# Mixture-of-experts stage: two experts' first products together, then two experts' second products; eight buffers weighted in place; sums in two banks

## The reference

```python
combine = (one_hot(topk_idx, 8) * softmax(topk_vals)[..., None]).sum(axis=1)   # 2 of 8 experts
h = relu(einsum('td,edh->teh', x_flat, W1) + b1)      # first product, hidden width 128
y = einsum('teh,ehd->ted', h, W2) + b2                # second product
out = einsum('ted,te->td', y, combine)             # weighted sum over the experts
```

## Time and profile before

| | us |
|---|---|
| median of 3 runs | 1169.35 (1168.31 to 1169.48) |
| the profiled execution's own time | 1169.17 |
| its span, first to last instruction | 1167.4 |
| PE busy over the span | 1102.7 (94%) |
| ACT busy | 794.0 (68%) |
| DVE busy | 694.9 (60%) |
| POOL busy | 142.1 (12%) |
| DVE line 2071 (`mult`), 64 | 78.2, mean 1.221 |
| ACT line 1269 (`relu`), 64 | 71.2, mean 1.113 |
| PE line 1679 (`second`), 256 instructions | 68.9 |
| a weight row from issue to landing, median of 64 | 7.8 |

### The profile page before, as it was taken

One profiled execution on the slowest core, in us unless ns is written; L12 is line 12 of the kernel. 1 busy time (PEld: TensorE's weight loads), 2 busy tenths in 40 slices (PEclk: granted clock), 3 DMA queues, 4 the chain that ended last, 5 costly groups with the idle time before them and its releaser, 6 DMA issues.

```text
span 1167.4 us, 62466 instructions
## 1 busy us (share of the span) xinstructions
PE 1102.7 (94%) x26872; PEld 930.9 (80%) x26872; DVE 694.9 (60%) x3130; ACT 794.0 (68%) x4592; POOL 142.1 (12%) x220
## 2 busy tenths in 40 slices
PE   3799999999999999999999999999798699889998
PEld 2699999999999999999999999999544388623332
DVE  7565455555555555555555554444456669899985
ACT  1466677777777777777777777666569888556654
POOL 4200000000000000000000000000104212412110
PEclk9555555555555555555555555555699989999999
DMA  5000000000000000000000000000000000448675
GB/s 141 8 9 9 9 12 11 10 9 9 9 14 10 9 9 9 14 10 9 9 5 4 5 4 4 4 4 5 2 1 1 1 1 1 147 160 287 216 261 173
DMA packets 30545, 47.20 MB, mean 40 GB/s; under 512 B 12274, under 2 KB 21563, under 8 KB 30268
## 3 DMA queue, kind: packets, MB, share of 16 engines
q1 hardware_dynamic: 30268, 43.21, 11.1%
HBM read 40.84 MB, written 2.36 MB: 37 GB/s over the span
## 4 chain that ended last, share of the span: by engine, by line
PE 83%; DVE 8%; ACT 4%; issue 2%; POOL 2%; DMA 1%; SPq 0%; DVEq 0%; ACTq 0%
PE bank L659 44%; PE bank L756 7%; PE bank L1386 5%; PE bank L739 5%; PE bank L1679 4%; PE bank L427 4%; PE bank L528 3%; PE bank L734 2%; PE bank L751 1%; DVE gp L2071 1%; POOL stat L1027 1%; PE bank L1584 1%; PE bank L412 1%; PE bank L1419 1%; PE bank L447 1%
## 5 line engine op out<-in xcount | busy, mean ns | idle before, releaser
L659 PE MATMUL bank<-space,whh_hi 128*128 128x8 f16 x16384 | 612.4, 170 | 7.2 <-DVE space L787 4.6
L659 PEld LDWEIGHTS bank<-space,whh_hi 128*128 128x128 f16 x16384 | 530.6, 105 | 28.0 <-DVE space L787 8.2
L787 DVE TENSOR_TENSOR space<-h_f,space 128x16 f16<-128x16 f32 x2048 | 290.6, 176 | 384.3 <-ACT h_f L768 383.0
L768 ACT ACTIVATE h_f<-bank 128x16 f32<-128x16 f32 x2048 | 298.5, 183 | 234.5 <-PE bank L659 228.4
L774 ACT ACTIVATE space<-bank 128x16 f16<-128x16 f32 x2048 | 298.0, 183 | 1.1 <-PE bank L659 1.1
L756 PE MATMUL bank<-space,wih_hi 128*128 128x32 f16 x2048 | 178.2, 188 | 0.0
L659 PE MATMUL bank<-space,whh_lo 128*128 128x32 f16 (+1 forms) x2096 | 145.2, 191 | 0.0
L739 PE MATMUL bank<-xr,wih_lo 128*128 128x32 f16 x512 | 123.6, 241 | 0.0
L427 PE MATMUL bank<-onehot,tab 128*128 128x128 f16 x448 | 116.7, 266 | 0.4 <-DVE prepare_cur L477 0.4
L756 PEld LDWEIGHTS bank<-space,wih_hi 128*128 128x128 f16 x2048 | 114.2, 104 | 0.0
L739 PE MATMUL bank<-xr,wih_hi 128*128 128x32 f16 x512 | 109.8, 215 | 0.0
(11 more groups left out here) (288 smaller groups left out, 1560.8 us busy)
## 6 DMA issues: line engine op xcount, KB each, us to landing
space<-weights_kept SPq DMA_DIRECT2D x64, 512.0 KB, 7.8
space<-in_x SPq DMA_DIRECT2D x28, 129.0 KB, 3.1
out<-res SPq DMA_DIRECT2D x8, 256.0 KB, 9.6
space<-in_wrec SPq DMA_DIRECT2D x1, 768.0 KB, 4.2
space<-in_wx SPq DMA_DIRECT2D x1, 740.5 KB, 9.4
brec<-in_brec SPq DMA_DIRECT2D x1, 260.0 KB
ew<-in_ew SPq DMA_DIRECT2D x1, 256.0 KB, 4.1
weights_kept<-wturned SPq DMA_DIRECT2D x8, 32.0 KB, 1.8
```

What stands on the lines that cost most here:

```text
L659: mm = pe.matmul(own[:, m, :], w[:, k, m * P:(m + 1) * P], steps(h, k), start=False, stop=False, skip_group_check=True)
L768: act.activation(h_f[layer][:, s % 2, :, :], own, ACT.Tanh, scale=scale[layer]).then_inc(s_h[layer], 1)
L787: dve.tensor_tensor(h[layer][:, :, s % RINGS[layer], 1, :], h_f[layer][:, s % 2, :, :], h[layer][:, :, s % RINGS[layer], 0, :], ALU.subtra ...
```

## The change

Six edits, all in the last stage:

1. PE takes slots in pairs (2k, 2k + 1): `hidden(2k + 2)`, `hidden(2k + 3)`, then `weights_turned` if due, `second(2k - 1)`, `second(2k)`, then the norm, gates or `sum_turned` of either slot.
2. `relu` and `mult` share eight buffers (`gel`, `gp`, and two old attention tiles, two slots each). `mult` writes over what it reads. `relu(n)` waits for `second(n - 8)` and no longer for a `mult`; `mult(n)` no longer waits for a `second`.
3. The expert sums of even sequences go to bank 2, of odd ones to bank 7; `second` waits for the copy of two sequences ago.
4. `sum_turned` writes to bank 3, which the norm also uses; the norm waits for `add_experts` of the sequence before, `sum_turned` for the norm's copy.
5. SP issues weight row e only when row e - 3 of the same sequence has landed.
6. The queues of ACT and DVE keep their order.

```diff
--- before.py
+++ after.py
@@ -902,7 +902,9 @@
         grank, gsel, gc = (tmp(n, [P, TT, NE]) for n in ("grank", "gsel", "gc"))
         gleft, wturned = tmp("gleft", [P, NE, TT]), tmp("wturned", [NE * TT, P])
         gr = gel[:, :, :, :].rearrange("p e h t -> p e (h t)")
-        weighted = gp[:, :, :, :].rearrange("p e h t -> p e (h t)")
+        gr_more = gp[:, :, :, :].rearrange("p e h t -> p e (h t)")
+        expert_at = lambda n: (gr, gr_more, rabs, phk)[n % 8 // 2][:, n % 2, :]
+        sum_bank = lambda b: bank[2 + b % 2 * 5]
         gst = tmp("gst", [P, 3, TT])
         wide = rph.rearrange("p (e t) -> p e t", e=NE)
         weight_rows = whole[0:NE, :]
@@ -947,6 +949,8 @@
                 if x == 0:
                     sp.wait_ge(s_phi, B)
                 for e in range(NE):
+                    if e >= 3:
+                        sp.wait_ge(s_wide_row[e - 3], 16 * (x + 1))
                     if x:
                         sp.wait_ge(s_gp, NE * (x - 1) + e + 1)
                     sp.dma_start(wide[:, e, :], kept[x, e].partition_broadcast(P)).then_inc(s_wide_row[e], 16)
@@ -1264,16 +1268,16 @@
 
             def relu(n):
                 act.wait_ge(s_hid, n + 1)
-                if n >= 2:
-                    act.wait_ge(s_gp, n - 1)
-                act.activation(gr[:, n % 2, :], banks[n % 2 * 2][:, :], ACT.Relu, bias=ebias[:, n % NE:n % NE + 1],
+                if n >= 8:
+                    act.wait_ge(s_sec, n - 7)
+                act.activation(expert_at(n), banks[n % 2 * 2][:, :], ACT.Relu, bias=ebias[:, n % NE:n % NE + 1],
                                scale=unscale[S_E1]).then_inc(s_r, 1)
 
             def sum_copy(b):
                 act.wait_ge(s_sec, NE * (b + 1))
                 if b:
                     act.wait_ge(s_moet, b)
-                act.activation(yt[:, :], bank[2], ACT.Copy).then_inc(s_moec, 1)
+                act.activation(yt[:, :], sum_bank(b), ACT.Copy).then_inc(s_moec, 1)
 
             for b in range(B):
                 if b == 6:
@@ -1664,30 +1668,30 @@
             def second(n):
                 b, e = divmod(n, NE)
                 if e == 0:
-                    if b:
-                        pe.wait_ge(s_moec, b)
+                    if b == 0:
+                        pe.wait_ge(s_lg, 2)
+                    elif b == 1:
+                        pe.wait_ge(s_wor, B)
                     else:
-                        pe.wait_ge(s_lg, 2)
+                        pe.wait_ge(s_moec, b - 1)
                     pe.wait_ge(s_wgt_rows, 16 * (b + 1))
                     for half in range(2):
-                        mm = pe.matmul(bank[2][half * D:(half + 1) * D, :], eb2[0:NE, :],
+                        mm = pe.matmul(sum_bank(b)[half * D:(half + 1) * D, :], eb2[0:NE, :],
                                        weight_rows[:, half * 512:(half + 1) * 512], start=True, stop=False,
                                        skip_group_check=True)
                     mm.then_inc(s_b2, 1)
                 pe.wait_ge(s_gp, n + 1)
                 for half in range(2):
-                    mm = pe.matmul(bank[2][half * D:(half + 1) * D, :], ew2[:, e, :], gp[:, n % 2, half, :],
-                                   start=False, stop=(e == NE - 1), skip_group_check=True)
+                    mm = pe.matmul(sum_bank(b)[half * D:(half + 1) * D, :], ew2[:, e, :],
+                                   expert_at(n)[:, half * 512:(half + 1) * 512], start=False, stop=(e == NE - 1),
+                                   skip_group_check=True)
                 mm.then_inc(s_sec, 1)
 
             def sum_turned(b):
                 pe.wait_ge(s_moec, b + 1)
-                if b:
-                    pe.wait_ge(s_fin, b)
-                else:
-                    pe.wait_ge(s_wor, B)
+                pe.wait_ge(s_xt, OPEN + B + min(b + 3, B))
                 for i in range(4):
-                    mm = pe.transpose(bank[7][:, i * P:(i + 1) * P], yt[:, i * P:(i + 1) * P], eye[:, :])
+                    mm = pe.transpose(bank[3][:, i * P:(i + 1) * P], yt[:, i * P:(i + 1) * P], eye[:, :])
                 mm.then_inc(s_moet, 1)
 
             for b in range(B):
@@ -1718,22 +1722,32 @@
                 project_out(b)
             gates(1, bank[2][:, 0:TT * NE])
 
-            for n in range(slots):
-                b, e = divmod(n, NE)
-                y, step = divmod(n + 3, NE)
-                if n + 1 < slots:
-                    hidden(n + 1)
-                if step == 7 and y + 1 < B:
-                    weights_turned(y + 1, bank[6][0:NE * TT, P:2 * P])
-                if n:
-                    second(n - 1)
-                if step == 0 and y + 1 < B:
-                    norm_turn(pe, bank[3], B + y + 1)
-                elif step == 1 and y + 1 < B:
-                    gates(y + 1, bank[6][:, 0:TT * NE])
-                if e == 3 and b:
-                    sum_turned(b - 1)
+            hidden(1)
+            for k in range(slots // 2):
+                pair = (2 * k, 2 * k + 1)
+                for n in pair:
+                    if n + 2 < slots:
+                        hidden(n + 2)
+                for n in pair:
+                    y, step = divmod(n + 3, NE)
+                    if step == 7 and y + 1 < B:
+                        weights_turned(y + 1, bank[6][0:NE * TT, P:2 * P])
+                for n in pair:
+                    if n:
+                        second(n - 1)
+                for n in pair:
+                    b, e = divmod(n, NE)
+                    y, step = divmod(n + 3, NE)
+                    if step == 0 and y + 1 < B:
+                        if b:
+                            pe.wait_ge(s_fin, b)
+                        norm_turn(pe, bank[3], B + y + 1)
+                    elif step == 1 and y + 1 < B:
+                        gates(y + 1, bank[6][:, 0:TT * NE])
+                    if e == 3 and b:
+                        sum_turned(b - 1)
             second(slots - 1)
+            pe.wait_ge(s_fin, B - 1)
             sum_turned(B - 1)
 
 
@@ -2062,18 +2076,15 @@
 
             def mult(n):
                 b, e = divmod(n, NE)
-                if n == 1:
-                    dve.wait_ge(s_att, B)
-                elif n >= 2:
-                    dve.wait_ge(s_sec, n - 1)
+                own = expert_at(n)
                 dve.wait_ge(s_r, n + 1)
                 dve.wait_ge(s_wide_row[e], 16 * (b + 1))
-                dve.tensor_tensor(weighted[:, n % 2, :], gr[:, n % 2, :], wide[:, e, :], ALU.mult).then_inc(s_gp, 1)
+                dve.tensor_tensor(own, own, wide[:, e, :], ALU.mult).then_inc(s_gp, 1)
 
             def add_experts(b):
                 dve.wait_ge(s_moet, b + 1)
                 own = res[:, span(b), 0:D].rearrange("p (h i) d -> p h i d", h=2)
-                dve.tensor_tensor(own, halves(bank[7]), own, ALU.add).then_inc(s_fin, 1)
+                dve.tensor_tensor(own, halves(bank[3]), own, ALU.add).then_inc(s_fin, 1)
 
             for n in range(slots):
                 b, e = divmod(n, NE)
```

## The result

| | before | changed |
|---|---|---|
| median of 13 runs each | 1169.82 (1168.31 to 1171.38) | 1171.95 (1170.72 to 1173.71) |
| ratio to before, 95% interval | | 1.0019 (1.0012 to 1.0027) |
| profiled execution, its span | 1169.17, 1167.4 | 1170.72, 1168.9 |

The changed kernel is slower by 2.1 us, 0.19%. The forecast was 1.9 us over its own reference, at 1171.2, in a range of 1163 to 1176. The interval lies above 1 and reaches over both sides of the 0.2% that I called no change; the ratio itself is just within it.

The account below looks back on a forecast made before the run. The prediction took TensorE as full (91.60 of 91.90 us) and DVE as nearly full; +4.8 - 0.7 - 2.2 = +1.9 gave 1171.1 against the profiled 1169.17, forecast as 1171.2 us, range 1163 to 1176.

Parts of the forecast that it names:

- middle: First norm to last norm, five sequences: 19.3 to 19.35 us each, 96.7 against 91.9, so +4.8 us.
- start: Up to the first norm: at 1029.55 against 1030.21, so -0.7 us, with bounds 0 and -1.2.
- tail: Last norm to the end: 42.3 us before, forecast 40.0 to 40.1, with a sum of -2.26.
- Seams: TensorE's switches between first and second products: 0.27 us for two; pairs save 0.93 a sequence, leaving 17.34 of own work.
- The hold behind the norm: H9, slot 9's first product, waits for a relu queued behind the norm's copy: TensorE stands still 1.43 us a sequence.
- The small stalls: Per sequence, TensorE loses 0.24 us at the sum copy (slots 12, 13) and 0.31 to DVE's chain (slot 15).
- The pacing: Weight rows by threes: cost taken as 0, bounds 0 and +4 us; the tail bears a trip of 5.2 at most.
- In place: DVE's weighting written over its input: cost taken as 0, bounds -0.02 and +0.02 us an instruction.
- (a): Rival: DVE is the bound, the norm's hold is hidden and the seams' saving comes through; 1161 us, chance 0.13.
- (b): Rival: a seam is the price of a semaphore wait, not of the shape; 1175 us, chance 0.10.
- (c): Rival: pacing of the rows starves DVE, shown by DVE waiting for rows in the last sequence; 1174.6 us, chance 0.11.
- (d): Rival: the pairs move nothing, since DVE is full and the holds fall in its shadow; 1169.2 us, chance 0.08.

Follow-up runs that it names:

- e5: The changed kernel with the bias product over all 128 rows (added rows zero) in place of 8; 1171.64 us, ratio to before 1.0022.
- e8: e7 without the pacing of the weight rows; 1160.61 us, ratio to before 0.9935.
- e1: The changed kernel with slot 7's relu ahead of the copy of the turned norm in ScalarE's queue; 1164.77 us, ratio to before 0.9958.
- e7: e1 with `third_high`, ScalarE's high half of the norm, moved behind slot 5's relu; 1161.07 us, ratio to before 0.9937.
- e3: The changed kernel, pairs kept, but relu and weighting with the old two plus two buffers and their old waits; 1180.85 us, ratio to before 1.0097.
- e4: The changed kernel without the wait of weight row e for row e - 3; 1171.32 us, ratio to before 1.0018.

## Why the prediction was right

Its three terms were +4.8 (middle), -0.7 (start) and -2.2 (tail), +1.9 in all. Measured between the two profiled executions: 96.62 - 91.85 = +4.77, 19.91 - 20.59 = -0.68, 40.04 - 42.31 = -2.27, +1.82. The medians of 13 runs differ by 2.13. The working took the 91.9 of the kernel before from the same execution, with the late rows in it; against sequences of 18.27 throughout the middle is +5.3, so half a microsecond of the agreement is luck. The terms' order of size and their causes hold:

- **Seams.** Eights of 1.89 to 1.95 came wherever a kind follows itself. e5 shows the shape as the cause at the bias product, the rows at `sum_turned` that the type has no part. TensorE's own work in a sequence is some 17.4 (e8's 17.64 less the 0.19 at the norm and 0.06 at slot 13), where 17.34 was worked out. The Trainium skill (TensorEngine Tiling (Array Packing), Tiling Modes) says that changing the tiling mode drains TensorE; e5's step from 1.00 to 0.86 agrees; what TensorE does in that time no row shows.
- **The hold behind the norm.** H9 was put at 2.73 and came at 2.74. e1 takes it away and gets 1.42 a sequence (19.32 to 17.90), as worked out (1.43).
- **The small stalls.** Their sum of 0.55 was near the measured 0.51, their sizes were not. 0.24 was put on the sum copy: H12 waits for nothing, and H13 loses 0.06 at most (1.95 for eight in place of 1.89), because the relu of slot 10 started 0.64 behind the copy in place of 0.75. 0.31 was put on DVE's chain: by the starts it costs 0.45, and e7 gets back 0.25 of it before DVE's queue holds the norm. The one makes up for the other by necessity and not by chance: DVE's chain reaches H15 at 16.39 whatever the sum copy does, so the 0.24 was never a term of its own, and the lower bound of 18.8, with neither stall, could come only with a shorter chain. With 17.4 + 1.42 + 0.06 + 0.45 the sequence is 19.33, against 19.32 measured.
- **The start.** -0.68 against -0.7, and by its cause: the relu of slot 5 no longer waits for a buffer, which e3 takes back whole.
- **The tail.** By the earlier trace rows and the rows above, TensorE's busy time there fell by 2.83 (the working had -0.86 - 2.43 + 0.30 = -2.99) and its idle time grew by 0.63 (+1.55 - 0.82 = +0.73). I had let the rows cost nothing there: the last row was just in time, and in e5's profiled execution it was not.
- **The pacing.** The limit named, a trip of 5.2 us for three rows in a chain 1, 4, 7, is what e1 runs into (4.86, 5.28, 5.22), though only once the hold is out of the way. I took 0, which was right for this kernel by that shadow.
- **In place.** DVE's weighting lasts 1.22 as before, so 0 was right.

The rivals fall thus: (a) by the norms of 19.32, though e8 shows its state to be reachable; (b) by e5; (c) by e4, though the sign that I had named for it, DVE waiting for rows in the last sequence, did come: that sign was badly chosen, since TensorE waits for none of those weightings, and two of the waits stay without the pacing; (d) by the distances, since the pairs move each of the three terms, and they nearly cancel. What the range held wider than needed was (a): it was argued from DVE's 17.2 of 18.38, which bounds a gain but does not bring it.

## What to carry to other kernels

When an engine's order is regrouped, walk the queues of the others against the new order: an instruction whose own operand is early can now stand behind one whose operand comes late, just where a regrouped engine wants it sooner, and here moving two such instructions took the ratio from 1.0019 to 0.9937, some 9.6 us. Grouping instructions of one shape saves what their seams cost, but the grouped instruction also asks earlier for its buffers. A pacing or a wait that costs nothing should be looked at again once the stall that shadows it is gone.

## What the runs showed of the hardware

A switch between products of 128 by 128 and 128 by 64, or between 8 and 128 rows with the same type, cost TensorE 0.10 to 0.15 us at a granted clock of 1.00, against 0.86 for the four matmuls of a group. A switch from f32 to f16 at the same shape cost nothing (0.11 from the last transpose to the first product, the pace of the transposes). I had not expected that filling the missing rows with zeros would be the cheaper product: between products over 128 rows it lay 0.86 from its follower with 128 rows, and 1.00 with 8.
